# Layer 0 of a two-layer graph kernel: a pair's edge lists are loaded one turn earlier, between two node loads

## What is computed

```
h = relu(layernorm(x))                                   # x: 12500 nodes x 64
x = x + relu(h @ W_self + mean_over_edges(h[src]) @ W_neigh + b)      # layer 0, 412500 edges
h = relu(layernorm(x))
x = x + layer1(h)      # edge MLP and gate, per-node sum and max, node MLP, residual
```

## Time and profile before

| | us |
|---|---|
| three runs | 7846.05, 7850.81, 7857.41 |
| median | 7850.81 |
| the profiled execution | 7891.66 |
| its span, first to last instruction | 7889.9 |
| layer 0's turns | from about 580 to 3170 |
| layer 1 | from about 3200 to the end |

### The profile page before, as it was taken

One profiled execution on the slowest core, in us unless ns is written; L12 is line 12 of the kernel. 1 busy time (PEld: TensorE's weight loads), 2 busy tenths in 40 slices (PEclk: granted clock), 3 DMA queues, 4 the chain that ended last, 5 costly groups with the idle time before them and its releaser, 6 DMA issues. The chain is left out here.

```text
span 7889.9 us, 109070 instructions
## 1 busy us (share of the span) xinstructions
PE 3888.9 (49%) x24783; PEld 3407.5 (43%) x24784; DVE 4369.9 (55%) x9411; ACT 1828.3 (23%) x3642; POOL 4131.3 (52%) x3884
## 2 busy tenths in 40 slices
PE   0006666777777767344344444444444444445442
PEld 0005655666666666233343333433433434444441
DVE  5775555555555554355555555555555555555552
ACT  4105555555555555000000000000000000000000
POOL 5234244445555444656555555665555555555545
PEclk9999888888888888555555555555555555555555
DMA  7100113222232222322222222322222222222221
GB/s 208 33 20 17 26 34 93 83 87 92 88 92 90 86 92 91 94 76 76 76 79 79 75 78 78 83 80 80 82 77 80 81 81 79 79 79 85 81 81 30
DMA packets 402218, 611.87 MB, mean 78 GB/s; under 512 B 191933, under 2 KB 274979, under 8 KB 402107
## 3 DMA queue, kind: packets, MB, share of 16 engines
q0 software_dynamic: 182688, 377.75, 17.8%
q1 hardware_dynamic: 150357, 130.12, 5.2%
q10 hardware_dynamic: 69094, 103.21, 4.4%
HBM read 470.99 MB, written 118.43 MB: 75 GB/s over the span
## 5 line engine op out<-in xcount | busy, mean ns | idle before, releaser
L567 POOL DMA_INDIRECT counts_f<-hA_table,stage x2496 | 2579.2, 1033 | 1960.4 <-issue 744.1
L1751 PE MATMUL ps_acc<-msg,ident 128*128 128x64 f32 (+1 forms) x4974 | 1271.9, 430 | 1207.5 <-DVE msg L1411 979.0
L1751 PEld LDWEIGHTS ps_acc<-msg,ident 128*128 128x128 f32 x4974 | 1121.5, 326 | 1357.9 <-DVE msg L1411 796.0
L1592 ACT ACTIVATE counts_f<-ps_pairs 128x784 bf16<-128x784 f32 x1568 | 1262.3, 823 | 1186.9 <-PE ps_pairs L1773 570.4
L1773 PE MATMUL ps_pairs<-hot 128*128 128x196 bf16 x6272 | 908.1, 273 | 762.9 <-ACT counts_f L1592 424.1
L1781 PE MATMUL ps_acc<-pieces_f,counts_f 128*128 128x192 bf16 x9604 | 1130.8, 263 | 11.0 <-ACT counts_f L1592 7.2
L567 POOL DMA_INDIRECT extra_f<-hA_table,estage x780 | 879.9, 1128 | 241.7 <-issue 241.7
L1781 PEld LDWEIGHTS ps_acc<-pieces_f,counts_f 128*128 128x128 bf16 x9604 | 976.4, 141 | 16.8 <-issue 11.8
L1773 PEld LDWEIGHTS ps_pairs<-hot 128*128 128x128 bf16 x6272 | 569.2, 104 | 930.4 <-issue 894.1
L1246 DVE TENSOR_TENSOR hot<-val,iota_lo 128x2048 bf16<-128x2048 bf16 x392 | 480.9, 1227 | 800.0 <-PE ps_pairs L1773 395.3
L1394 DVE TENSOR_TENSOR pre<-counts_f,own 128x512 f32 (+1 forms) x854 | 592.5, 694 | 489.5 <-issue 431.9
(11 more groups left out here) (239 smaller groups left out, 3139.3 us busy)
## 6 DMA issues: line engine op xcount, KB each, us to landing
early_rows<-extra_f SPq DMA_DIRECT2D x196, 384.0 KB
counts_f<-early_rows ACTq DMA_DIRECT2D x98, 768.0 KB
counts_f<-hA_table,stage POOLq DMA_INDIRECT x2496
counts_f<-counts_f SPq DMA_DIRECT2D x78, 288.0 KB
own<-own_rows ACTq DMA_DIRECT2D x98, 128.0 KB
extra_f<-hA_table,estage POOLq DMA_INDIRECT x780
hA_table<-node ACTq DMA_DIRECT2D x98, 96.0 KB
sorted_rows<-srt SPq DMA_DIRECT2D x14, 252.0 KB, 2.6
```

Source lines behind the costliest of these rows:

```text
L567: return pool.indirect_dma_start(to, None, table, bass.IndirectOffsetOnAxis(ap=idx, axis=axis))
L1592: act.activation(counts[:, c, nodes, :].rearrange("p (b h) t -> p b (h t)", h=2), ps_pairs[g & 1][:, :].rearrange("p (b w) -> p b w", b=BA ...
L1751: return pe.matmul(ps_sum[:, 0:D], ident[:, :], rows, start=False, stop=False, skip_group_check=True)
```

## The change

`next_tiles(q)` now begins with the node load of the first tile, then waits until the index rows of pair q are made and loads the edges of pair q+1, and only then waits for the second `s_x1` and loads the second tile's nodes. The edges of pairs 0, 1 and 2 are loaded ahead of the first turn, and the last turn, which has no edges left to load, is written out behind the loop.

```
-            def next_tiles(q):
-                wait_alone(sp, s_prep, q * 2)
-                for c in range(2):
-                    load_edges(q * 2 + c, c)
-                for c in range(2):
-                    wait_alone(sp, s_x1, q * 2 + (c - 3))
-                    load_nodes(q * 2 + (c - 2), c)
+            def next_tiles(q, edges=True):
+                wait_alone(sp, s_x1, q * 2 - 3)
+                load_nodes(q * 2 - 2, 0)
+                if edges:
+                    wait_alone(sp, s_prep, q * 2 + 2)
+                    for c in range(2):
+                        load_edges(q * 2 + (c + 2), c)
+                wait_alone(sp, s_x1, q * 2 - 2)
+                load_nodes(q * 2 - 1, 1)
...
             sp.wait_ge(s_prep, 2)
             for t in range(2, 4):
                 load_edges(t, t & 1)
+            sp.wait_ge(s_prep, 4)
+            for t in range(4, 6):
+                load_edges(t, t & 1)
...
-            with in_one_block(sp, 6 + TITER, TPAIRS) as q:
+            with in_one_block(sp, 6 + TITER, TPAIRS - 1) as q:
                 next_tiles(q)
                 for e in range(GROUP_PIECES):
                     store_early(q - 2, e)
+            next_tiles(TPAIRS - 1, edges=False)
+            for e in range(GROUP_PIECES):
+                store_early(TPAIRS - 3, e)
```

## The result

| | runs | median us | lowest to highest |
|---|---|---|---|
| before | 13 | 7835.01 | 7805.31 to 7860.2 |
| after | 13 | 7904.02 | 7863.26 to 7936.76 |

The ratio is 1.0091, with a 95% interval of 1.0075 to 1.0107: the change makes the kernel 69 us slower. The profiled execution of after took 7919.61 us, against 7891.66 before.

What follows compares the result with a forecast made beforehand. No engine is full; layer 0's turn is a loop of waits, PE's signals late while gathers and SP's DMAs overlap. -15.3 + 39 + 22 = +46 us on 7850.8 gives 7897 us, range 7870 to 7920 (8 in 10: 7800 to 7940).

Steps and rivals of the forecast that it cites:

- Three waits go: DVE at edge_ids in layer 0: three waits for edge loads vanish, -15.3 us at most, 0 as the other end.
- The burst: First half of a turn: five small loads instead of three beside POOL's eight gathers lengthen ACT's gaps, +39 us over 35 turns.
- tips short turns into long ones: Layer 0's turns: some short turns (mean 50.5 us) become long ones (mean 55.2 us), +22 us.
- 1.1 us a turn: Short turn's first-half gaps of 1.56 us, grown by 0.92 / 1.30; +39 us over 35 turns.
- the quarter that the forecast took: Share of the 23 short turns taken to become long: 6 x (4.7 - 1.1) = +22 us.
- Rival A: The two loads in the first half are absorbed; only the 15.3 us or part go: 7836 to 7851 us; chance 0.26.
- Rival B: Faster by more than the waits, as edge loads leave their place before the gathers: 38 us, 7813 us; chance 0.30.
- the condition: At edge_ids: unprofiled runs wait more often than three times in 36; 5 us every third turn gives another 45 us, 7770.
- Its other reading: In the three turns with a wait, edge loads run into gathers; each saves its wait and 9.2 - 1.6 = 7.6 us.
- Rival C: Layer 0's turns: the five-load burst tips every short turn into a long one, +93 us, 7944 us; chance 0.10.
- D: SP's queue: if s_prep came later, the second node load would be held and DVE's mean_of would wait; chance under 0.01.

Runs made afterwards that it cites:

- all_quiet_again: After, but from pair 13 node loads, edge loads and stores wait for the first half's gathers, second tile's nodes behind the stores; first kind: 7750.84 us, ratio 0.9887.
- extra_new: Before, plus two unused loads a turn between the node loads, where the change moves the edges; edges stay; second kind: 6330.49 us, ratio 0.9998.
- after_again: The changed kernel itself, unaltered, run next to before on the second kind of chip: 6088.41 us, ratio 0.9627 to before.
- all_quiet: After, but from pair 13 node loads, edge loads and stores wait for the first half's gathers, second tile's nodes behind the stores; second kind: 6083.94 us, ratio 0.962.

## Why the prediction was right

It gave 7897 us, slower, with 7870 to 7920 as its own range; measured were 7904. The absolute figure came out closer than the change did: 46 us were forecast and 69 measured, but the forecast stood on the median of three runs, 7850.8, and the median of all 13 is 7835.0. That part is luck. The direction and the place are not; the way in which its two costs share the sum is again in part luck.

- *Three waits go, -15.3 us.* None is left but the first. Whether 15.3 us were gained is not shown: the waits stood behind second halves that were not late, and after has only one of these. That turn (2521.86 to 2564.96) takes 43.1 us, where the two clear cases of before took 48.4 and 48.0 with a wait of 4.5, so the price of one wait seems right.
- *The burst makes the first half's gaps longer, +39 us, and tips short turns into long ones, +22 us.* The direction, the place and the mechanism are as forecast: gaps over 1.5 us beside and behind the five loads, the count over 54 us up from 12, the mean turn up. The shares are not. 11 turns stayed short and went from a mean of 50.5 to 51.4 us, about +10 us; 12 more turns became long, at 54.9 - 50.5 = 4.4 us each, +53 us; the 12 long ones went from 55.2 to 54.9 us, -4. Together that is the 59 us of the profile. So 1.1 us a turn was a fair price for a turn that stays short, but it was counted for all 35, and the tipping was 12 of 23 and not the quarter that the forecast took. That quarter rested on the turn with the wait at 2629.74, where node loads stand beside the gathers too, and the error in one term made up for that in the other.
- *Is it the loads beside the gathers?* The counts of late first halves (one of 29 with no small load, 11 of 32 with three, 22 of 34 with five), and the six turns of all_quiet_again in which node loads meet the gathers after all, show that small loads there delay the copies. all_quiet_again moves node loads and stores too, so it is no measure of the edges alone. That the two edge loads alone cost 69 us on this kind of chip was not shown, and neither was it ruled out that the new order of the waits has a part in it; both runs made for it fell on the other kind.
- *Rival A (absorbed)* is out for the first kind. On the second kind two loads in the new place cost nothing that shows (ratios 0.9998 and 1.0001).
- *Rival B (faster)* had the condition: it would be more if there were more such waits, since DVE's slack is smaller than what it waits "remote". On the second kind there is nothing "remote", the wait is there in all 35 turns, and the change gains 235 us (variants of it up to 240). That condition was right, and its size (5 us in every third turn, 7770) fitted no chip. Its other reading, that the waits' turns lose 7.6 us more because the edge loads run into the gathers, is not borne out: in all_quiet_again three node loads alone do as much there (10.1 to 10.4 us in sum).
- *Rival C* (all turns long, 7944) is out: 24 of 35 are. *D* is out: among the waits of after there is no row in which DVE waits for `xh`.

The rule of the Trainium skill that the prediction weighed (page "DMA: Bandwidth & Descriptors", section "Issuing engines are not separate DMA queues": DMAs started by different engines run on the same DMA engines and interleave) gives no price for a small load beside a gather. By it alone the prediction had -15 us. On the first kind of chip the change cost 69 us, on the second two loads more or fewer a turn changed nothing (ratios 0.9998, 1.0001 and 1.0006).

**What stays open.** What makes PE's signals arrive late on one kind of chip and not on the other. The instructions of ACT and DVE take the same time on both (a copy 823 ns, a one-hot row 1785 ns); what differs are the gaps. They come in steps of about 0.7 us (0.7, 1.5, 2.1, 2.9, 3.6, 4.2, 4.9), for which no run gives a reason. Nor is this a matter of layer 0 alone: of the 1581 us between the spans of before (7889.9) and extra_new (6309.1), 1197 lie behind the last `edge_ids`, in layer 1 above all. There the kernel before has "remote" waits too, on the first kind (the largest, from 3200 to 7880 us, is shown), and extra_new has none from 2800 to 6300 us:

```profile
DVE msg L1411 <- remote: 728.9, 114, 18.1
```

## What to carry to other kernels

A load that an early turn needs must not stand behind stores that wait for this turn's last work: that can close a loop, and here one load left there kept all of it closed. Whether such a loop is the bound can depend on the chip, so look at how much slack the wait has, and what would take that slack away; a profile in which the wait is rare may hide it behind another delay. When a load must move, put it where no gathers run: here that version (7751 and 6084 us) beats the kernel before on both kinds of chip, and on the second it is as fast as the change itself. And read a forecast's terms by class: a mean of 52.1 us was made of turns of 50.5 and 55.2, and what moved was mostly how many there are of each.

## What the runs showed of the hardware

- Same program, same inputs, two kinds of chip: 7835 to 7842 us on one, 6319 to 6332 on the other, 24% apart, and one change with opposite signs. In the slower one idle time marked "remote" stands before ACT (120 times in 35 turns of after) and DVE (70 times), beside gathers of POOL; in the faster one the same turns have no such row (extra_new, after_again).
- On the first kind the delay goes with what else is issued. Beside eight gathers the median gap of a copy is 0.7 to 0.9 us with no small load and with three, and 1.6 to 2.2 us with five; late first halves (6.8 us and more in sum; with loads, those behind a second half in time left out) number one of 29, 11 of 32 and 22 of 34. Beside twelve gathers and the stores the first gap is 3.0 us with the node loads there and 1.5 us without, the next are 2 to 5 us in all three.
- PE's mean granted clock in layer 0's turns is 0.83 before and after the earlier trace rows and 0.87 in all_quiet_again on the first kind, 0.92 in extra_new and 0.96 in all_quiet on the second: in these runs it is higher where PE idles less (busy 1315 of 1824 us in before, 1155 of 1309 in all_quiet).
